# A hand-ordered transformer block on one core: another instruction order on four engines, sigmoid from silu, and low halves moved from VectorE to GpSimd

## What is computed

```
    x = x + _L0_attn_ref(_layernorm(x, axis=-1), ...)
    x = x + _L0_ffn_ref(_layernorm(x, axis=-1), ...)
# attention
        energy = jnp.einsum('bnd,bne->bde', K, V)
        context = jnp.einsum('bnd,bde->bne', Q, energy)
# experts
        scores = jax.nn.sigmoid(x @ Wr)
        _, idx = lax.top_k(scores + router_bias, TOP_K)
        hid = jax.nn.silu(g) * u
        mlp_out = jnp.einsum('tei,eih->teh', hid, Wd)
        routed = jnp.einsum('te,teh->th', cw[:, :E_MLP], mlp_out)
        shared = lax.conv_general_dilated(hidden_states, conv_w, ..., feature_group_count=Hd) + conv_b
```

## Time and profile before

| | |
|---|---|
| median of 3 runs | 894.48 us (891.71 to 897.38) |
| the profiled execution | 893.6 us, of which the span from first to last instruction is 891.8 us |
| PE busy | 855.9 us, 96% |
| DVE busy | 741.1 us, 83% |
| ACT busy | 628.7 us, 71% |
| POOL busy | 572.7 us, 64% |
| granted TensorE clock, mean | 0.989 |

### The profile page before, as it was taken

How to read it: one execution, slowest core, us unless ns; L and a number is a source line. 1 busy time by engine, 2 the same in 40 slices (tenths; PEclk the granted TensorE clock), 3 DMA queues, 4 the chain that set the end, 5 groups by cost and what they waited for, 6 DMA issues and landing times.

```text
span 891.8 us, 16729 instructions
## 1 busy us (share of the span) xinstructions
PE 855.9 (96%) x5437; PEld 754.3 (85%) x5437; DVE 741.1 (83%) x2056; ACT 628.7 (71%) x1238; POOL 572.7 (64%) x654
## 2 busy tenths in 40 slices
PE   5789999999999999999999999999999999999997
PEld 4668989898888888988889888888888898788876
DVE  5758889988888998888898888899888887767775
ACT  5676777777687777778677777777777775655643
POOL 3336776667676657667666767666576766556663
PEclk9989999999999999999999999999999999999999
DMA  9111434543334543343544343454424344433333
GB/s 286 57 52 47 137 121 142 143 117 99 95 119 142 144 142 68 114 129 120 143 143 114 101 115 99 143 144 142 119 72 119 101 114 119 111 104 100 106 91 84
DMA packets 79446, 103.86 MB, mean 116 GB/s; under 512 B 6528, under 2 KB 58880, under 8 KB 79360
## 3 DMA queue, kind: packets, MB, share of 16 engines
q1 hardware_dynamic: 74752, 86.02, 30.4%
q0 software_dynamic: 4608, 16.78, 10.0%
HBM read 68.96 MB, written 17.04 MB: 96 GB/s over the span
## 4 chain that ended last, share of the span: by engine, by line
PE 66%; DVE 13%; POOL 12%; issue 5%; ACT 4%; DMA 0%; POOLq 0%; ACTq 0%; DVEq 0%
PE ps_gu L406 9%; PE ps_gu L408 9%; PE ps_gu L407 9%; POOL enx L1368 7%; PE ps_y L406 5%; PE ps_y L408 5%; PE ps_y L407 5%; PE ps_sh L543 4%; PE ps_sh L533 3%; POOL gate L1327 3%; PE ps_sh L516 2%; DVE stats L1065 2%; DVE acc L1057 2%; ACT x L840 2%; PE ps_y L456 2%
## 5 line engine op out<-in xcount | busy, mean ns | idle before, releaser
L1327 POOL TENSOR_TENSOR gate<-gate,cwb 128x512 f32<-128x512 f32 x128 | 167.5, 1309 | 127.8 <-ACT gate L763 126.4
L406 PE MATMUL ps_gu<-x2T_hi,wgu_hi 128*128 128x512 f32 x512 | 212.2, 414 | 0.0
L408 PE MATMUL ps_gu<-x2T_hi,wgu_lo 128*128 128x512 f32 x512 | 203.0, 396 | 0.0
L407 PE MATMUL ps_gu<-x2T_lo,wgu_hi 128*128 128x512 f32 x512 | 202.2, 395 | 0.0
L1368 POOL TENSOR_TENSOR enx<-inv_e,logits 128x32 f32<-128x32 f32 x32 | 177.5, 5546 | 8.6 <-ACT logits L756 8.6
L406 PE MATMUL ps_y<-wd_hi,hid_hi 128*128 128x256 f32 x512 | 152.8, 299 | 4.0 <-DVE hid_lo L1018 3.1
L1029 DVE SCALAR_TENSOR_TENSOR conv<-x2T,conv_w,conv 128x512 f32<-128x512 f32 x192 | 146.4, 801 | 0.0
L408 PE MATMUL ps_y<-wd_hi,hid_lo 128*128 128x256 f32 x512 | 145.3, 284 | 0.0
L407 PE MATMUL ps_y<-wd_lo,hid_hi 128*128 128x256 f32 x512 | 144.2, 282 | 0.0
L1011 DVE TENSOR_TENSOR hid<-ps_gu,gate 128x512 f32<-128x512 f32 x128 | 86.0, 672 | 39.2 <-POOL gate L1327 38.1
L408 PEld LDWEIGHTS ps_gu<-x2T_hi,wgu_lo 128*128 128x128 f32 x512 | 96.9, 189 | 22.5
(11 more groups left out here) (115 smaller groups left out, 1934.3 us busy)
## 6 DMA issues: line engine op xcount, KB each, us to landing
cwb<-cw_rows SPq DMA_DIRECT2D x128, 256.0 KB, 4.0
xa<-in_x SPq DMA_DIRECT2D x32, 512.0 KB, 7.5
acc<-in_x SPq DMA_DIRECT2D x32, 512.0 KB, 6.7
acc<-x POOLq DMA_DIRECT2D x32, 512.0 KB, 4.6
out<-acc SPq DMA_DIRECT2D x64, 256.0 KB, 2.3
cwb<-in_wg SPq DMA_DIRECT2D x4, 128.0 KB, 4.0
cwb<-in_wu SPq DMA_DIRECT2D x4, 128.0 KB, 3.8
cwb<-in_wd SPq DMA_DIRECT2D x1, 512.0 KB, 4.5
```

The source lines that it names most:

```text
L406: nc.tensor.matmul(dst, a_hi, b_hi, start=start, stop=False, skip_group_check=True)
L407: nc.tensor.matmul(dst, a_hi, b_lo, start=False, stop=False, skip_group_check=True)
L408: return nc.tensor.matmul(dst, a_lo, b_hi, start=False, stop=stop, skip_group_check=True)
L1327: g.tensor_tensor(gate[:, e % 2], gate[:, e % 2], cwb[:, q, e], ALU.mult).then_inc(gatew_ready, 1)
```

## The change

Nothing of the arithmetic of the products changes. Three things do:

- **Sigmoid.** `power` on POOL goes. ACT now also copies the absolute value of the logits, DVE takes its maximum with a tiny number (`magnitude`), ACT takes silu of minus that (`score_dip`), and `route` on DVE begins with a reciprocal, a product and two short instructions that turn it into the sigmoid.
- **Low halves.** `hid_low` of experts 1 and 2 and `xn_low` move from DVE to POOL (`gate_low`, `xn_low`), beside the one of expert 3 that POOL had.
- **Order.** On PE `conv_transpose` and the first down product come after `gate_up(st, 5)` and not after `gate_up(st, 4)`, and the attention products come ahead of them, except in a step with a chain. On DVE `hidden(st, 0)` stands right behind the first taps, the sums of the first norm behind the second taps, and the residual and the second norm's sums ahead of `hidden(st, 2)` and `route`. ACT and POOL are ordered to suit.

The diff, cut:

```diff
@@ -713,22 +715,18 @@
                     gate_up(st, 3)
                 if m_on:
                     chain_f(st)
-                if b_on and drain:
+                elif b_on:
                     attention(st, 0)
                 if c_on:
                     gate_up(st, 4)
-                if b_on and drain:
+                if b_on and not m_on:
                     attention(st, 1)
                 if c_on:
+                    gate_up(st, 5)
                     conv_transpose(st)
                     down(st, "C", 0)
-                if b_on and not m_on and not drain:
+                if m_on:
                     attention(st, 0)
-                if c_on:
-                    gate_up(st, 5)
-                if m_on:
-                    attention(st, 0)
-                if b_on and not drain:
                     attention(st, 1)
                 if c_on:
                     gate_up(st, 6)
...
                 copy(logits[:, :], ps_sh[0][:, 0:TG * NE]).then_inc(logits_ready, 1)
+                nc.scalar.activation(size[:, :], ps_sh[0][:, 0:TG * NE], ACT.Abs).then_inc(logits_ready, 1)
...
+            def score_dip(st):
+
...
+                nc.scalar.activation(dip[:, :], mag[:, :], ACT.Silu, scale=-1.0).then_inc(dip_ready, 1)
...
             def body(st):
                 c_on, r_on, m_on = st.on("C"), st.on("R"), st.chain()
                 if m_on:
                     gram_copy(st)
                 if c_on:
...
                 if st.on("A"):
                     xn_split(st)
-                if c_on:
+                if r_on:
+                    x2T_out(st, 0)
+                if m_on:
+                    gramT_copy(st)
+                elif c_on:
+                    hid_high(st, 0)
+                if r_on:
+                    x2T_out(st, 1)
+                if m_on:
+                    p1_copy(st)
+                if c_on:
+                    silu(st, 1)
+                if m_on:
+                    et_copy(st)
+                    hid_high(st, 0)
...
+                if c_on:
+                    hid_high(st, 1)
                     silu(st, 2)
...
+                    skip_part(st)
...
@@ -973,10 +993,10 @@
                     hid_high(st, 2)
                 if st.on("L"):
                     norm1(st)
+                if st.on("B") and not m_on:
+                    norm2(st)
                 if r_on:
                     weights_copy(st)
-                if st.on("B") and st.drain():
-                    norm2(st)
...
-            def xn_low(st):
...
-                v.tensor_tensor(xn_lo, xn[:, st.slot("A", 4)], xn_hi.bitcast(F32), ALU.subtract)\
-                    .then_inc(xnlo_ready, 1)
...
+            def magnitude(st):
...
+                v.tensor_scalar(mag[:, :], size[:, :], LEAST, None, ALU.max).then_inc(mag_ready, 1)
...
+                dve.wait_ge(mag_ready, st.before("R", 1, 1))
+                done(v.reciprocal(rmag[:, :], mag[:, :]))
+                dve.wait_ge(dip_ready, st.before("R", 1, 1))
+                after()
+                done(v.tensor_tensor(minor[:, :], dip[:, :], rmag[:, :], ALU.mult))
+                after()
+                done(v.scalar_tensor_tensor(signed[:, :], logits[:, :], 0.0, minor[:, :], ALU.is_gt, ALU.add))
+                after()
+                done(v.scalar_tensor_tensor(flat(score[:, :, :]), signed[:, :], -1.0, signed[:, :], ALU.mult, ALU.max))
...
@@ -1229,43 +1256,37 @@
                 if c_on:
                     dve.wait_ge(halo_ready, st.before("C", 1, 1))
                     conv_tap(st, 0)
+                    hidden(st, 0)
+                if r_on:
+                    x2T_low(st, 0)
+                if c_on:
+                    conv_tap(st, 1)
+                if r_on:
+                    x2T_low(st, 1)
                 if st.on("L"):
                     norm1_stats(st)
-                if r_on:
-                    x2T_low(st, 0)
-                if c_on:
-                    conv_tap(st, 1)
-                if r_on:
-                    x2T_low(st, 1)
+                if c_on:
+                    hid_low(st, 0)
+                if r_on:
+                    magnitude(st)
+                if c_on:
+                    hidden(st, 1)
                 if y_on:
                     output(st, 0)
                     output(st, 1)
                 if c_on:
-                    hidden(st, 0)
                     conv_tap(st, 2)
-                    hid_low(st, 0)
-                    hidden(st, 1)
-
                 if m_on:
                     f_low(st)
-                drain = st.drain()
-                if c_on:
-                    hid_low(st, 1)
-                if st.on("A"):
-                    xn_low(st)
-                if b_on and drain:
+                elif b_on:
                     residual(st, 0)
                     residual(st, 1)
                     norm2_stats(st)
-                if r_on and c_on and not b_on:
+                if c_on:
+                    hidden(st, 2)
+                if r_on:
                     route(st)
-                if c_on:
-                    hidden(st, 2)
-                if r_on and c_on and b_on:
-                    route(st)
-                if c_on:
-                    hid_low(st, 2)
-                if b_on and not drain:
+                if m_on:
                     residual(st, 0)
                     residual(st, 1)
                     norm2_stats(st)
...
+            def gate_low(st, e):
+
...
+                g.tensor_tensor(hid_lo[:, k], hid[:, k], hid_hi[:, k].bitcast(F32), ALU.subtract)\
+                    .then_inc(hidlo_ready[k], 1)
...
+            def xn_low(st):
...
+                g.tensor_tensor(xn_lo, xn[:, st.slot("A", 4)], xn_hi.bitcast(F32), ALU.subtract)\
+                    .then_inc(xnlo_ready, 1)
...
-            def power(st):
...
-                g.tensor_tensor(enx[:, :], inv_e[:, :], logits[:, :], ALU.pow).then_inc(enx_ready, 1)
...
-                g.tensor_tensor(den[:, :], enx[:, :], one_e[:, :], ALU.add).then_inc(den_ready, 1)
...
             def body(st):
-                c_on, r_on = st.on("C"), st.on("R")
+                c_on, r_on, b_on, m_on = st.on("C"), st.on("R"), st.on("B"), st.chain()
                 if c_on:
                     gate_weight(st, 0)
+                if st.on("A"):
+                    xn_low(st)
+                if c_on:
                     gate_weight(st, 1)
-                if r_on:
-                    power(st)
-                if c_on:
+                norm1_factors(st)
+                if c_on:
+                    gate_low(st, 1)
                     gate_weight(st, 2)
-                    norm1_factors(st)
-                    if st.drain():
-                        relu_add(st)
-                        if st.on("B"):
-                            norm2_factors(st)
+                if b_on and not m_on:
+                    norm2_factors(st)
+                if c_on:
+                    gate_low(st, 2)
                     gate_weight(st, 3)
-                if c_on and not st.drain():
                     relu_add(st)
-                if st.on("B") and not st.drain():
+                if m_on:
                     norm2_factors(st)
                 if c_on:
-                    last_low(st)
+                    gate_low(st, 3)
                 if r_on:
                     skip_factors(st)
```

More of the change, by code:

```diff
@@ L188, in program @@
         logits = sb("logits", [P, TG * NE])
-        enx = sb("enx", [P, TG * NE])
-        den = sb("den", [P, TG * NE])
+        size = sb("size", [P, TG * NE])
+        mag = sb("mag", [P, TG * NE])
+        dip = sb("dip", [P, TG * NE])
+        rmag = sb("rmag", [P, TG * NE])
+        minor = sb("minor", [P, TG * NE])
+        signed = sb("signed", [P, TG * NE])
         score = sb("score", [P, TG, NE])
@@ L583, in attention @@
                 else:
-                    pe.wait_ge(logits_ready, st.before("R", 1, 1))
+                    pe.wait_ge(logits_ready, st.before("R", 2, 2))
                 if h == 0:
@@ L928, in head, with skip_part, relu_part @@
                 xnT_high(at("A", 5, NG), 1)
+            def skip_part(st):
+                q = st.slot("C", 2)
+                act.wait_ge(skip_ready, st.before("C", 2, 2))
+                for t in range(TG):
+                    a = acc[:, st.slot("C", 4), t]
+                    nc.scalar.activation(a, a, ACT.Identity, bias=skip_bias[:, q, t:t + 1],
+                                         scale=skip_scale[:, q, t:t + 1]).then_inc(ident_added, 1)
+            def relu_part(st):
+                q = st.slot("C", 2)
+                act.wait_ge(cw_ready, st.before("C", 1, 1))
+                for t in range(TG):
+                    nc.scalar.activation(x2[:, q, t], x2[:, q, t], ACT.Relu, scale=cw[:, q, EM + 3, t:t + 1])\
+                        .then_inc(relu_ready, 1)
             def body(st):
@@ L1072, in flat @@
                 return t.rearrange("p t e -> p (t e)")
+            def magnitude(st):
```

(9 more changed lines are left out.)

64 lines of the change are left out of this document (24 added, 40 removed).

## The result

The changed kernel takes 1111.3 us (median of 4 runs, 1106.91 to 1114.92) beside 894.6 us for the kernel before: 1.2415 times as long, 95% interval 1.2381 to 1.2449. The forecast was 944 us with a range to 985. The sign was right, the size far too small: 217 us more instead of 50.

A forecast was written before the change was run, and what follows sets the result against it. PE was taken as the bound, its waits lost in full: 893.6 us plus 44 (plain steps), 3 (chain steps) and 3 (drain) gave 943.6, plus 0.9 to the median, 944.5 us; range 896 to 985.

The forecast's parts named there:

- The bound: Full steps: PE sets the pace, reordering other engines gains nothing, and any PE wait is lost in full.
- the prediction's own signs: Plain step 26.5 to 28.5 us, PE's longest wait conv_transpose; waits at routing weights would mean the place is wrong.
- The convolution's wait: PE waits for DVE's convolution in every plain step, 2.2 us (1.0 to 3.3), 44 us over 20 steps.
- Due: When PE, undisturbed, would reach conv_transpose in a plain step: 11.34 us after its start before, 2.35 us later after.
- The first wait: DVE's hidden(st, 0), behind the first taps, waits 1.4 us for POOL's first routing weight.
- one hold: DVE's last taps are held by one POOL instruction, 0.86 us; up to 2 us if a second slips in.
- the spare of 1.2 us: Plain step: time between the last taps' end at 494.23 and PE reaching the convolution at 495.41, to cover DVE's waits.
- The rule that was weighed there: VectorE instructions with two SBUF inputs contend with GpSimd ones reading SBUF; the second to issue fully blocks.
- That start stays where it is: DVE's work for the convolution still begins at 482.97, after ACT's last transposed half of the normed input.
- The clock: Rival: PE waits trigger up to 20 lower-clock spells of 1.7 us, 34 us more, 978 us; chance 0.16.
- The drain: Drain steps, where PE waits for DVE's routing weights: +3 us, with ends of -10 and +6.
- The sigmoid: Two new ACT instructions hide in waits for PE; route's three more DVE instructions, some 0.3 us each, count in the drain.

The follow-up runs named there:

- e1: Changed kernel with GpSimd's DMA relu_add issued one piece earlier, right behind the third routing weight: 981.7 us.
- e4: Kernel before, its order and low halves kept, with the new sigmoid alone (power gone): 904.6 us.
- e11: Changed kernel, relu_add one piece earlier, all three moved low halves back on VectorE, ScalarE's hid_high(st, 0) behind x2T_out(st, 1) in steps without a chain: 924.7 us.
- e3: Changed kernel with xn_low and the low halves of experts 1 and 2 back on VectorE: 1051.9 us.
- e5: Changed kernel with relu_add one piece earlier and xn_low and the low halves of experts 1 and 2 back on VectorE: 929.7 us.
- e6: Changed kernel with relu_add one piece earlier and, of the moved low halves, xn_low alone back on VectorE: 959.4 us.

## Why the prediction fell short

**The bound** was right: PE sets the pace, nothing was gained in the full steps, and PE's idle time grew by 143.9 us of waits. The count of the steps was off by one: of the 26 full steps seven hold a chain, and 19 are plain. By the prediction's own signs the place was wrong: a plain step of up to 28.5 us was forecast, the one shown took 34.28, and PE's largest wait hangs on the routing weights.

**The convolution's wait** was right in its mechanism and nearly in size, the latter in part by luck. Due: 13.7 us after the step's first `gate_up` by the earlier trace rows and the three moved pieces; measured 733.23 - 715.58 = 17.65 us, less the two waits of 1.17 and 2.60, 13.9. The first wait was put at 1.4 us and took 1.48. `xn_low` was put at 2.4 us and took 2.36; it held the second taps by 0.91 us (2.30 - 1.39 in the earlier trace rows), not 1.1. The last taps were given one hold of 0.86 us and had both, 1.96 us (3.35 - 1.39); the upper value in the text, 2 us, was the one to take, since the weight is queued right behind the low half. With the spare of 1.2 us these make 3.2 us and not 2.2. Besides, DVE's work starts later, as shown below. PE's wait of 1.17 us at the router, ahead of the convolution, took up a part of all this, and 2.60 us were left. In e1, without the late copy, the wait is 2.6 us in 15 of the 19 plain steps. The full steps of the changed kernel (from 81.07 to 931.51) come to 44.9 us, where 44 were forecast for the plain steps and 3 for those with a chain, which have none:

```profile
PE ps_y L459 <- DVE conv L1049: 44.9, 19, 2.6
```

The other 10.4 us of the 55.3 lie in the drain and the tail.

The rule that was weighed there (the Trainium skill, SBUF — State Buffer, Who interferes with whom) says that the second of two such instructions is fully blocked. The held pairs agree: `xn_low` ends at 723.85, and with a free pair's 1.39 us the taps would end at 725.24; they ended at 725.06. On the power, where the rule and the row differed, the row was right: with it gone in the old order (e4), the mean tap went from 801 to 769 ns and the time went up.

**The step that failed** is the sentence "That start stays where it is, since ACT's copies just ahead of it stand in the same order". The copies do, among themselves; but the change puts `norm2` ahead of them, and that edit was priced nowhere. In the step shown, DVE's start (717.85) is 2.27 us behind the first `gate_up` (715.58); in the kernel before it was 1.25 us (482.97 - 481.72 in the earlier trace rows). `norm2` waits for GpSimd's DMA, whose issue stands behind the fourth `gate_weight`. The wait of 65.5 us at `xn_transpose`, and by e1 some 130 us of the result, hang on this. The data was at hand: the diff shows `norm2` jump the copy; it also shows that the kernel before issued `relu_add` early in the drain, where `norm2` stood early too, and that the change drops this special case. What the moved `norm2` waits for, the landing of a DMA on another engine's queue, was not followed up.

**The clock** was left out of the sum and priced as a rival at 34 us, on the ground that one of two equal waits had kept its clock. (Of the two spells in the drain that it names, the one at 864.70 us came 0.7 us behind a wait of 1.68 us for a low half; the routing weights had cost 0.3 us there.) With waits of some 3 and 2.5 us at two places in a step the busy time of the same matmuls grew by 73.6 us, a third of the loss. No spells follow where nothing waits: before, the full steps ran at 1.00. A forecast that adds waits by the dozen has to carry this term in its sum.

**The drain** was put at +3 us and lost 40.1. There too `norm2` waits for the DMA, x2 is late, and PE waits up to 3.2 us for it at the router; and the taps are held as in the full steps. e1 alone brings the drain from 159.0 to 131.8 us. **The ACT order** at the router had no term in the sum. PE's wait there for x2T, 18.3 us, is mostly the late norm's again, since e1 leaves 5.6. In the step shown the rounding of `hidden(st, 0)`, now ahead of the second half of x2T, stood 2.06 us for DVE just before, so it passed that wait on to PE. That this order costs time by itself is not shown: e11, which turned it round, removed the row, but not the time.

**The sigmoid** was taken as free in the steps, where e4 puts 2.5 us on it, and stood in the drain's +3 us; it cost 10, of which 7 in the drain.

## What to carry to other kernels

When an engine's call moves ahead of another, list what the moved call waits for, down to the landing of DMAs that another engine issues, and who waits for the calls that it now stands in front of; a copy of 0.25 us behind a late norm cost more than all the moved arithmetic. Where PE is the bound, price a wait twice: for its length, and for the slower clock that can follow. Work that is moved from VectorE to a less busy GpSimd isn't free: three low halves cost 25 us in one order and 52 in another.

## What the hardware showed

- The wait for a DMA's landing stood in the waits as "issue", for 132.2 us in 23. The time from issue to landing, 4.5 to 5.6 us in 32, told who released it, and moving the DMA's issue (e1) took the row away. In e3 three such waits, 19.8 us, do carry the DMA's name.
- A VectorE instruction on 128x4 elements can be held like a tap: in the changed kernel `wsum_eps` took 1.27 us and ended at 706.97, beside a low half on GpSimd from 705.64 to 706.94; in e5 it took 0.17 us at 710.94.

```profile
705.70 1.27 DVE L1132 TENSOR_SCALAR wsum_eps<-wsum 128x4 f32<-128x4 f32 x1
```

- In e6, 16 waits of 1.6 us for the convolution left the clock of the full steps at 0.99; in e1, with 19 waits of 2.3 us, it was 0.96. In e5 seven spells at the lower level followed waits at the router of 0.8 us at most, and other such waits had no spell behind them. What sets a spell off was not told apart.
